# fc2's rescale over two PSUM banks at once, y's high halves on VectorE, g's normalising and h's cast on GpSimd, and attention jobs three steps apart

## The reference, cut to what matters

```python
x = L0_attn_x                                   # (4, 2048, 512) f32
xn = _layernorm(x)
# linear-attention recurrence over the 2048 steps, M is 128 x 128
#   r_t = q_t @ M.T ;  M = 0.99 * M + v_t.T @ k_t / b
s = (retrieved @ Wo.T) * sigmoid(gate)
h = _layernorm(xn) * ln_gamma + ln_beta
y = silu(h @ dequant(fc1_q, fc1_scales) + fc1_bias)    # 512 -> 2048
z = y @ dequant(fc2_q, fc2_scales) + fc2_bias          # 2048 -> 512
out = x + s * silu(xn + 0.5 * z)
```

## Time and profile before

| | |
|---|---|
| time, median of 3 runs | 1356.86 us (1355.76 to 1358.03) |
| profiled execution | 1356.22 us, of it 1354.4 us from first to last instruction |
| mean granted TensorE clock | 0.973 of full speed; 1.00 in each stretch between 120 and 1300 us |
| TensorE busy | 1227.3 us, 91% |
| VectorE busy | 1076.9 us, 80% |
| ScalarE busy | 1032.3 us, 76% |
| GpSimd busy | 608.7 us, 45% |
| HBM traffic | 48 GB/s over the span |

### The profile page before, as it was taken

How to read it: one execution, slowest core, us unless ns; L and a number is a source line. 1 busy time by engine, 2 the same in 40 slices (tenths; PEclk the granted TensorE clock), 3 DMA queues, 4 the chain that set the end, 5 groups by cost and what they waited for, 6 DMA issues and landing times.

```text
span 1354.4 us, 18593 instructions
## 1 busy us (share of the span) xinstructions
PE 1227.3 (91%) x5888; PEld 588.1 (43%) x5888; DVE 1076.9 (80%) x1829; ACT 1032.3 (76%) x1805; POOL 608.7 (45%) x638
## 2 busy tenths in 40 slices
PE   0359999999999999999999999999999999999993
PEld 0124444444444444444444444444444444444441
DVE  6758979788787978878797877879787887978686
ACT  1547788788788878778787878878887887878782
POOL 4145652717154271816437181643718163362623
PEclk8579999999999999999999999999999999999997
DMA  8601021120302111030212103030211203020111
GB/s 277 233 1 32 1 63 32 47 47 8 87 1 62 33 51 44 13 82 1 74 21 56 39 18 76 1 81 14 62 33 29 65 1 93 2 63 0 38 26 32
DMA packets 41620, 65.68 MB, mean 48 GB/s; under 512 B 11696, under 2 KB 11952, under 8 KB 41008
## 3 DMA queue, kind: packets, MB, share of 16 engines
q1 hardware_dynamic: 41232, 64.36, 18.2%
q10 hardware_dynamic: 288, 0.08, 0.0%
HBM read 47.59 MB, written 16.81 MB: 48 GB/s over the span
## 4 chain that ended last, share of the span: by engine, by line
PE 61%; ACT 22%; issue 10%; DVE 3%; POOL 2%; DMA 1%; SPq 0%; ACTq 0%; POOLq 0%; DVEq 0%
PE blk L447 22%; PE blk L465 20%; PE side L408 9%; ACT blk L550 8%; PE side L432 4%; ACT y_full L557 4%; ACT h_full L512 3%; PE side L424 2%; PE side L417 2%; ACT g_hi L506 2%; ACT y_split L565 2%; ACT z_rows L573 1%; PE side L426 1%; PE side L425 1%; DMA xt<-in_x 1%
## 5 line engine op out<-in xcount | busy, mean ns | idle before, releaser
L680 DVE TENSOR_TENSOR blk<-blk,ratio_rows 128x512 f32<-128x512 f32 x960 | 647.4, 692 | 182.7 <-PE blk L465 180.3
L550 ACT ACTIVATE blk<-blk,ratio 128x512 f32<-128x512 f32 x768 | 519.8, 683 | 181.5 <-PE blk L447 176.1
L447 PE MATMUL blk<-h_split,q_sb 128*128 128x512 f16 x2048 | 614.4, 382 | 43.8 <-ACT q_sb L591 29.0
L465 PE MATMUL blk<-w_sb,y_split 128*128 128x512 f16 x2048 | 609.4, 380 | 6.4 <-POOL w_sb L968 5.6
L465 PEld LDWEIGHTS blk<-w_sb,y_split 128*128 128x128 f16 x2048 | 199.6, 98 | 251.4 <-issue 6.9
L447 PEld LDWEIGHTS blk<-h_split,q_sb 128*128 128x128 f16 x2048 | 183.1, 98 | 289.4 <-ACT blk L550 80.2
L951 POOL TENSOR_TENSOR h_split<-h_full,h_split 128x512 f16<-128x512 f32 x64 | 81.7, 1276 | 478.5 <-DVE h_split L656 464.0
L557 ACT ACTIVATE y_full<-blk,par,last 128x512 f32<-128x512 f32 x256 | 204.6, 799 | 73.5 <-PE blk L447 72.5
L671 DVE SCALAR_TENSOR_TENSOR y_split<-y_full,up,y_split 128x512 f16<-128x512 f32 x256 | 222.5, 869 | 0.0
L565 ACT ACTIVATE y_split<-y_full,up 128x512 f16<-128x512 f32 x256 | 190.7, 745 | 0.0
L999 POOL TENSOR_TENSOR z_rows<-z_rows,s_rows 128x512 f32<-128x512 f32 x62 | 79.0, 1274 | 63.6 <-ACT z_rows L573 63.6
(11 more groups left out here) (131 smaller groups left out, 988.1 us busy)
## 6 DMA issues: line engine op xcount, KB each, us to landing
xt<-in_x SPq DMA_DIRECT2D x64, 256.0 KB, 4.6
x_again<-in_x SPq DMA_DIRECT2D x256, 64.0 KB, 1.9
out<-z_rows SPq DMA_DIRECT2D x256, 64.0 KB, 1.7
w_sb<-in_q SPq DMA_DIRECT2D x4, 1024.0 KB, 14.1
ratio_rows<-ratio_dram SPq DMA_DIRECT2D x4, 1024.0 KB, 15.5
y_split<-in_q SPq DMA_DIRECT2D x1, 1024.0 KB, 10.4
h_split<-in_q SPq DMA_DIRECT2D x1, 1024.0 KB, 12.6
z_rows<-in_q SPq DMA_DIRECT2D x1, 1024.0 KB, 14.3
```

What stands on the lines that cost most here:

```text
L447: mm = pe.matmul(blk[J % 2][:], q1_sb[:, g, j // 4, w, j % 4 * P:(j % 4 + 1) * P], a[:, c % 2, g, :], start=(g == 0 and n == 0), stop=(g = ...
L465: mm = pe.matmul(blk2[i][:], y[:, J % Y_RING, rows], w2_sb[:, j, part, :], start=(j == 0 and n == 0), stop=(j == FB - 1 and n == len(terms ...
L550: act.activation(blk[J % 2][:], blk[J % 2][:], ACT.Copy, scale=ratio1[:, at:at + 1]).then_inc(blk_scaled, 1)
L680: dve.tensor_tensor(blk2[i][:], blk2[i][:], ratio2_rows[:, j, :], ALU.mult).then_inc(blk2_scaled, 1)
```

## The change

It does five things.

- The four fc2 banks become one tensor of four banks. `block2_out` runs only after odd tiles and rescales (or writes to `z_rows`) two tiles, 128x1024 over two banks, in one instruction; the row of ratios is read twice by a broadcast. All counts of `blk2_scaled` and `z_out` are halved.
- `y_high` moves from ScalarE to VectorE, as a multiplication by the scale column, one step after silu, ahead of `y_low`, which comes two steps after silu instead of three.
- From the second chunk on, g's normalising (at steps 36, 38, 40, 42) and h's cast `h_high` move to GpSimd; the cast stands just ahead of `h_low`, three steps after the turn. The first chunk's stay on VectorE, with semaphores of their own.
- Jobs of a tile stand at 0, 4, 7, 10, 13 from its start instead of 0, 4, 6, 8, 11, so that wo comes one step after the next tile's qkv (for the last tile one step ahead of the first turn). Turns are at 51, 54, 56, 59 instead of 49, 52, 55, 58.
- `h_whole` is two steps after its turn for all four, `g_low` three.

```diff
-TILE_AT, JOB_AT = (1, 13, 25, 37), (0, 4, 6, 8, 11)
-TURN_AT = (49, 52, 55, 58)
-QKV_LAG, QKT_LAG, R_LAG, S_LAG, GHIGH_LAG, HFULL_LAG = 1, 1, 1, 1, 1, (2, 2, 2, 3)
+TILE_AT, JOB_AT = (1, 13, 25, 37), (0, 4, 7, 10, 13)
+TURN_AT = (51, 54, 56, 59)
+QKV_LAG, QKT_LAG, R_LAG, S_LAG, GHIGH_LAG, HFULL_LAG = 1, 1, 1, 1, 1, 2
 GATE_AT = (16, 17, 21, 29)
-STATS_AT, MOMENTS_AT, NORMALISE_AT = (0, 1, 2, 3), (5, 6), (33, 34, 37, 40)
-MASK_LAG, MEM_LAG, SPLIT_LAG, YHIGH_LAG, YLOW_LAG = 1, 1, (3, 3, 3, 4), 1, 3
-HLOW_LAG = 5
+STATS_AT, MOMENTS_AT = (0, 1, 2, 3), (5, 6)
+MASK_LAG, MEM_LAG, GLOW_LAG, YHIGH_LAG, YLOW_LAG = 1, 1, 3, 1, 2
+HSPLIT_LAG = 3
+NORMALISE_AT = (36, 38, 40, 42)
...
-        return NT * ((FB - 1) * c + j) + i + 1
+        return 2 * ((FB - 1) * c + j) + i // 2 + 1
...
-        blk2 = [ctx.enter_context(nc.psum_tensor(f"blk2_{n}", [P, T], F32)) for n in range(KC)]
+        blk2 = ctx.enter_context(nc.psum_tensor("blk2", [P, NT, H], F32))
         side = [ctx.enter_context(nc.psum_tensor(f"side{n}", [P, T], F32)) for n in range(2)]
-        first_turn_bank = blk2
+        first_turn_bank = [blk2[:, k, :] for k in range(KC)]
...
-                    mm = pe.matmul(blk2[i][:], y[:, J % Y_RING, rows], w2_sb[:, j, part, :],
+                    mm = pe.matmul(blk2[:, i, :], y[:, J % Y_RING, rows], w2_sb[:, j, part, :],
...
-            def y_high(J):
-                if J == 0:
-                    act.wait_ge(y_scaled, 1)
-                act.wait_ge(silu_done, J + 1)
-                wait(act, blk2_done, NT * (J - Y_RING + 1))
-                act.activation(y_hi[:, J % Y_RING, :], y_full[:, J % 2, :], ACT.Copy, scale=up_y
-                               ).then_inc(y_hi_done, 1)
...
-                for k in range(KC):
-                    at = job_behind(G, HFULL_LAG[k], "turn")
-                    if at and at[1] == k:
-                        h_whole(*at, side[JOB_BANK[G - HFULL_LAG[k]]])
+                if at := job_behind(G, HFULL_LAG, "turn"):
+                    h_whole(*at, side[JOB_BANK[G - HFULL_LAG]])
...
-            def normalise(c, i):
+            def first_h_high(k):
+                dve.tensor_copy(h_hi[:, 0, k, :], h_full[:, k % 2, :]).then_inc(first_h_hi_done, 1)
+            def first_normalise(i):
                 if i == 0:
-                    dve.wait_ge(rows_done, c + 1)
-                    wait(dve, turn_done, 4 * c)
-                dve.tensor_scalar(g_rows[:, i, :], xt[:, i, :], mv[:, c % 2, i, 0:1],
-                                  gs[:, c % 2, i:i + 1], ALU.subtract, ALU.mult).then_inc(g_done, 1)
+                    dve.wait_ge(rows_done, 1)
+                dve.tensor_scalar(g_rows[:, i, :], xt[:, i, :], mv[:, 0, i, 0:1],
+                                  gs[:, 0, i:i + 1], ALU.subtract, ALU.mult).then_inc(first_g_done, 1)
...
                 dve.tensor_tensor(g_lo[:, k, :], bank[:], g_hi[:, k, :], ALU.subtract).then_inc(g_lo_done, 1)
-            def h_high(c, k):
-                if k == 0 and c >= 2:
-                    dve.wait_ge(blk_done, FC1_COUNT[FB * (c - 1) - 1, KC - 1])
-                dve.tensor_copy(h_hi[:, c % 2, k, :], h_full[:, k % 2, :]).then_inc(h_hi_done, 1)
...
+            def y_high(J):
+                dve.wait_ge(silu_done, J + 1)
+                wait(dve, blk2_done, NT * (J - Y_RING + 1))
+                dve.tensor_scalar(y_hi[:, J % Y_RING, :], y_full[:, J % 2, :], up_y, None, ALU.mult
+                                  ).then_inc(y_hi_done, 1)
             def y_low(J):
...
             def block2_out(J, i):
                 c, j = divmod(J, FB)
+                pair = blk2[:, i - 1:i + 1, :]
+                scales = ratio2_rows[:, j, :].unsqueeze(1).to_broadcast([P, 2, H])
                 dve.wait_ge(blk2_done, NT * J + i + 1)
-                if c == 0 and i == 0 and j % 4 == 0:
+                if c == 0 and i == 1 and j % 4 == 0:
                     dve.wait_ge(ratio2_in[j // 4], 16)
                 if j < FB - 1:
-                    dve.tensor_tensor(blk2[i][:], blk2[i][:], ratio2_rows[:, j, :], ALU.mult).then_inc(blk2_scaled, 1)
+                    dve.tensor_tensor(pair, pair, scales, ALU.mult).then_inc(blk2_scaled, 1)
                 else:
-                    wait(dve, out_free[i], 64 * c)
-                    dve.scalar_tensor_tensor(z_rows[:, i, :], blk2[i][:], unit2[:, 0:1], ratio2_rows[:, j, :],
+                    for n in (i - 1, i):
+                        wait(dve, out_free[n], 64 * c)
+                    dve.scalar_tensor_tensor(z_rows[:, i - 1:i + 1, :], pair, unit2[:, 0:1], scales,
                                              ALU.mult, ALU.mult).then_inc(z_out, 1)
             def tail_sum(c, i):
-                dve.wait_ge(z_out, NT * c + i + 1)
+                dve.wait_ge(z_out, 2 * c + i // 2 + 1)
...
-            dve.tensor_copy(mix[:, 1:2], up_y).then_inc(y_scaled, 1)
...
                 ahead = c < NCH - 1
-                if at := fc2_step(G):
+                if (at := fc2_step(G)) and at[1] % 2 == 1:
                     block2_out(*at)
                 if at := job_behind(G, MASK_LAG, "scores"):
                     mask_scores(*at, side[JOB_BANK[G - MASK_LAG]])
-                for k in range(KC):
-                    at = job_behind(G, SPLIT_LAG[k], "turn")
-                    if at and at[1] == k:
-                        g_low(*at, side[JOB_BANK[G - SPLIT_LAG[k]]])
-                        h_high(*at)
+                if at := job_behind(G, GLOW_LAG, "turn"):
+                    g_low(*at, side[JOB_BANK[G - GLOW_LAG]])
                 if at := job_behind(G, MEM_LAG, "read"):
                     remember(*at, side[JOB_BANK[G - MEM_LAG]])
+                if (at := fc1_step(G - YHIGH_LAG) if G >= YHIGH_LAG else None) and at[1] == KC - 1:
+                    y_high(at[0])
...
-                if ahead and e in NORMALISE_AT:
-                    normalise(c + 1, NORMALISE_AT.index(e))
...
+            def normalise(c, i):
+                if i == 0:
+                    pool.wait_ge(rows_done, c + 1)
+                    pool.wait_ge(turn_done, 4 * c)
+                pool.tensor_scalar(g_rows[:, i, :], xt[:, i, :], mv[:, c % 2, i, 0:1],
+                                   gs[:, c % 2, i:i + 1], ALU.subtract, ALU.mult).then_inc(g_done, 1)
+            def h_high(c, k):
+                pool.wait_ge(h_full_done, 4 * c + k + 1)
+                if k == 0 and c >= 2:
+                    pool.wait_ge(blk_done, FC1_COUNT[FB * (c - 1) - 1, KC - 1])
+                pool.tensor_copy(h_hi[:, c % 2, k, :], h_full[:, k % 2, :]).then_inc(h_hi_done, 1)
             def h_low(c, k):
-                pool.wait_ge(h_hi_done, 4 * c + k + 1)
+                if c == 0:
+                    pool.wait_ge(first_h_hi_done, k + 1)
+                else:
+                    pool.wait_ge(h_hi_done, 4 * (c - 1) + k + 1)
...
-                if at := job_behind(G, HLOW_LAG, "turn"):
+                if c < NCH - 1 and e in NORMALISE_AT:
+                    normalise(c + 1, NORMALISE_AT.index(e))
+                if at := job_behind(G, HSPLIT_LAG, "turn"):
+                    h_high(*at)
```

More of the change, by code:

```diff
@@ L295, in wait, with g_wait @@
                 eng.wait_ge(s, count)
+        def g_wait(eng, c):
+            if c == 0:
+                eng.wait_ge(first_g_done, NT)
+            else:
+                eng.wait_ge(g_done, NT * c)
         def by_pool(c, i):
@@ L354, in _ @@
                 if c < NCH - 1:
-                    sp.wait_ge(g_done, 4 * c + 4)
+                    g_wait(sp, c)
                     load_x(c + 1)
@@ L388, in turn @@
                 if k == 0:
-                    pe.wait_ge(g_done, 4 * c + 4)
+                    g_wait(pe, c)
                 for i in range(NT):
@@ L454, in ffn2 @@
                 if j == 0:
-                    wait(pe, z_out, NT * (c - 1) + i + 1)
+                    wait(pe, z_out, 2 * (c - 1) + i // 2 + 1)
                 else:
@@ L610, in _ @@
                         silu(at[0])
-                if (at := fc1_step(G - YHIGH_LAG) if G >= YHIGH_LAG else None) and at[1] == KC - 1:
-                    y_high(at[0])
                 if at := job_behind(G, QKV_LAG, "qkv"):
@@ L794, in _ @@
             for i in range(NT):
-                normalise(0, i)
+                first_normalise(i)
             dve.wait_ge(all_tops_done, 1)
@@ L812, in _ @@
                 g_low(0, n - 1, first_turn_bank[n - 1])
[L813 removed]
+                first_h_high(n - 1)
                 last = top_of_q1(n)
@@ L817, in _ @@
             g_low(0, 3, first_turn_bank[3])
-            h_high(0, 3)
+            first_h_high(3)
             hold(0, s1_c, FB, KC)
```

11 lines of the change are left out of this document (6 added, 5 removed).

## The result

The changed kernel takes 1367.47 us (median of 4 runs, 1365.8 to 1370.01) where the kernel before takes 1356.34 beside it: 1.0082 times the time, interval [1.0062, 1.0101]. It is slower by 0.8%; forecast was 1347, 0.7% faster. The profiled execution's span is 1366.6 us, 12.25 more than before. One of the four executions of f2, an experiment further down, took 2592.86 us; f2's ratio is without it, its median (1328.1) with it.

The account below looks back on a forecast made before the run. TensorE was taken as the bound, with 5.8 us of holes in a 78.5 us chunk. Tile stretch 1.5 better, turn stretch 0.8 worse: 0.7 a chunk, 10 us in all, median 1347; forecast 1333 to 1354, full range 1314 to 1374.

Parts of the forecast that it names:

- tile stretch: The other 50 us of a chunk, outside the turns and next statistics: holes from 3.2 to 1.7, 1.5 us better.
- ScalarE's 0.15: Hole left near step 18, where two gate silus and the copy of wo meet: about 0.15 us a chunk.
- about 0.9 around step 20: One pair held where z's pairs, a y_high and a y_low meet GpSimd's prepares and sums: about 0.9 us.
- read 0.45 over three tiles: In the tile stretch, reads still waiting for the mask behind a pair: 0.45 us a chunk.
- room: Spare time before fc2 waits for a paired rescale: 0.7 us, where a single rescale has 2.1.
- turn stretch: From 686 to 711, the turns, then the next chunk's statistics, with VectorE the bound: 0.8 us worse a chunk.
- half a chunk: Gain counted over 15.5 chunks: the last has no turns, and the first's tiles wait for weights for a while.
- the tail: At the end, z of tiles 2 and 3 waits for the tail's sum, and two y_high: +1 us.
- The port's rule: Every y_high and y_low that begins beside GpSimd waits out its instruction; a caught y_low takes 1.36 us, not 0.73.
- The sum: 0.7 us a chunk over 15.5 chunks gives 11, less 1 at the end: 10 us gained, median 1347.
- VectorE takes over: Rival: caught instructions use up the pair's room, 1.4 us worse a chunk: 1378, or 1363 with fewer catches; chance 0.28.
- The port hardly bites: Rival: new halves miss GpSimd too, gaining 3.2 us a chunk: 1307, or partly so 1325; chance of below 1333 0.22.

Follow-up runs that it names:

- f2: The changed kernel with a tile's attention jobs at 0, 3, 6, 9, 13 steps instead of 0, 4, 7, 10, 13: 1328.1 us.
- c1: The changed kernel with GpSimd's output instructions, and VectorE's of the tail, on 4 of 512 columns: 1315.33 us.
- a2: The changed kernel with g's normalising back on VectorE: 1363.36 us.
- a5: The changed kernel with GpSimd's normalising as multiply and add, using two more row steps: 1366.27 us.
- g2: The changed kernel with single rescales, q2's widening two steps later and a tile's jobs at 0, 3, 6, 9, 13: 1296.22 us.
- a1: The changed kernel with y_high back on ScalarE and y_low a step later: 1340.26 us.

## Why the prediction was wrong

- **The step that failed is the tile stretch**, "1.5 us better": it came out 0.3 worse. ScalarE's 0.15 there is 0.16. The pair held "about 0.9 around step 20" is 1.16. The term that failed is "read 0.45 over three tiles": 2.19, of it 1.56 at step 35. The forecast let the mask wait for a pair, but not for a y_high of 1.31 and a pair that was itself late. It counted catches one by one, where y_high and y_low stand next to each other and are caught together: the pair is then 2.2 late, against a room that it had put at 0.7. In a middle chunk six y_low and two y_high are caught, where before four y_low were. Without GpSimd's wide work (c1) the three reads wait 0.6, near the 0.45 of the forecast.
- **The turn stretch** was forecast 0.8 worse and came out 0.1 better (2.5 for 2.6), so this error went the other way. Holes are at steps 11, 59 and 63, not at 4 and 6. Nor was h ever late.
- **The first chunk** was left out of the sum but for "half a chunk": +8.2. Without it the kernel would still have been 4 us slower. The slot of wo was noted for a gate silu's sake, and the queue that it was moved behind in the first chunk, `remember` behind the casts of q2, was not read.
- **Sizes.** Pairs 1.22 for 1.24, y_high 0.48 alone and up to 1.3 beside GpSimd (one of 1.41 in the first chunk), the tail +1.2 for +1: right. ScalarE's busy time fell by 138 us, not by 190: its records overlap, and the forecast took their full length. GpSimd's normalising 2.15 for 0.76: wrong, hidden in the middle chunks, and dear in the first (a2, a5).
- **The port's rule** was taken too widely: not every half that begins beside GpSimd waits it out. A y_high of 678.61 (0.48) and a y_low of 680.14 (0.74) lie within two normalisings of GpSimd (677.53 to 681.66) and are not stretched, nor is any half of the chunk in c1, where the normalisings stay whole.
- **The sum** is 22 us off by the profiled span: 12 in the second to last chunk (0.2 lost in place of 0.7 won, 15 times, less 1.2 in the second chunk), 8.6 in the first, 1.0 for the later start.
- **The rivals.** "VectorE takes over" named 1363 to 1378, and its mechanism (a pair's room used up by caught instructions) is the one found, but it made 0.2 a chunk and not 1.4; the rest is the first chunk, so that it named the right time is in part luck. "The port hardly bites" named 1307 to 1325, and c1, which takes most of GpSimd's work away, ran at 1315: a middle chunk 2.85 under before's for its 3.2, so its price was about right and its condition not met. (In c1's time the slow first chunk and the emptied tail nearly cancel.)

Left open: by which order of VectorE's queue the mask's slot wins its 0.8 with singles (g2), and how much of a1's 1.87 a chunk is y_high's move alone, since each kernel that takes it back also puts y_low a step later.
